# Splitting a matmul burst four and four, and moving ScalarE's exponential ahead of a PSUM bank's emptying, in a graph-attention kernel

## The reference, cut to what matters

```python
def gat_layer(x, graph, W, b):
    h = x @ W
    s = jnp.einsum('bnd,bmd->bnm', h, h) * graph
    s = jnp.where(s == 0.0, NEG_INF, s)
    a = jax.nn.softmax(s, axis=2)
    return jnp.einsum('bnm,bmd->bnd', a, h) + b
heads = jax.vmap(lambda W, b: gat_layer(flow_x, graph, W, b))(Wh, bh)      # 8 heads, 64 -> 128
x = jax.nn.leaky_relu(cat, negative_slope=0.01)                            # cat: the heads side by side
out = gat_layer(x, graph, W_out, b_out)
...
x = _layernorm(x + _L1_gnn_ref(x, adj, L1_gnn_Wh, L1_gnn_bh, L1_gnn_W_out, L1_gnn_b_out), axis=-1)
```

## Time and profile before

| | |
|---|---|
| median of 3 runs | 3353.29 us (3348.22 to 3355.03) |
| profiled execution: its own time, its span | 3351.83 us, 3349.9 us |
| busy: PE, DVE, ACT, POOL | 91%, 87%, 71%, 31% of the span |
| mean granted TensorE clock | 0.976 of full speed |
| the stage of the heads | from the first W product at 386 us to the last at 2101 us |
| DVE idle before L633, in all | 43.2 us, of it 39.8 us until PE's L594 |
| PE idle before L608, in all | 30.8 us, of it 29.6 us until ACT's L672 |
| ACT idle before L831, in all | 163.5 us, all of it until PE's L775 |

### The profile page before, as it was taken

How to read it: one execution, slowest core, us unless ns; L and a number is a source line. 1 busy time by engine, 2 the same in 40 slices (tenths; PEclk the granted TensorE clock), 3 DMA queues, 4 the chain that set the end, 5 groups by cost and what they waited for, 6 DMA issues and landing times. The chain is left out here.

```text
span 3349.9 us, 48846 instructions
## 1 busy us (share of the span) xinstructions
PE 3056.5 (91%) x15035; PEld 1842.5 (55%) x15035; DVE 2925.6 (87%) x3723; ACT 2393.7 (71%) x3653; POOL 1022.2 (31%) x709
## 2 busy tenths in 40 slices
PE   7998899999999999999999999799598888888857
PEld 3676566556665556665656655599454333333323
DVE  3478999999999999999999999688657999999844
ACT  0122688888888888888888888677246999999831
POOL 0123111111111111111111111000125999999821
PEclk9999999999999999999999999899799999999978
DMA  4000000100011111100010111000000000000001
GB/s 98 1 0 1 13 19 19 21 21 19 19 19 19 19 22 19 19 19 19 19 22 19 19 19 19 4 1 0 9 1 0 0 1 1 1 1 0 2 1 25
DMA packets 67230, 46.00 MB, mean 14 GB/s; under 512 B 48464, under 2 KB 49744, under 8 KB 67152
## 3 DMA queue, kind: packets, MB, share of 16 engines
q1 hardware_dynamic: 61920, 43.87, 6.7%
q10 hardware_dynamic: 5232, 1.12, 0.2%
HBM read 42.61 MB, written 2.36 MB: 13 GB/s over the span
## 5 line engine op out<-in xcount | busy, mean ns | idle before, releaser
L661 ACT ACTIVATE hid_work<-hid_work,hid_nmax 128x1024 f32<-128x1024 f32 x512 | 591.1, 1154 | 139.5 <-DVE hid_nmax L645 137.2
L633 DVE TENSOR_TENSOR hid_work<-hid_score_ps,A 128x1024 f32<-128x1024 f32 x512 | 619.5, 1210 | 43.2 <-PE hid_score_ps L594 39.8
L645 DVE CUSTOM_DVE_ANT_0 hid_work<-hid_masks,hid_work 128x1024 f32<-128x1024 f32 x512 | 631.4, 1233 | 0.2 <-DVE hid_masks L653 0.2
L1741 POOL TENSOR_TENSOR el<-el,node_edge 128x1024 f32<-128x1024 f32 x256 | 610.7, 2386 | 18.8 <-DVE el L1723 12.9
L889 POOL TENSOR_TENSOR leaky<-leaky,sloped 128x512 f32<-128x512 f32 x128 | 164.9, 1288 | 1312.5 <-DVE hid_masks L653 1293.5
L608 PE MATMUL hid_turn_ps<-ident,hid_work 128*128 128x128 f32 x4096 | 537.0, 274 | 30.8 <-ACT hid_probsT L672 29.6
L672 ACT COPY hid_probsT<-hid_turn_ps 128x512 f32<-128x512 f32 x1024 | 544.1, 587 | 0.0
L608 PEld LDWEIGHTS hid_turn_ps<-ident,hid_work 128*128 128x128 f32 x4096 | 470.0, 141 | 129.2 <-ACT hid_probsT L672 55.9
L815 PE MATMUL hid_mix_ps<-hid_probsT,x_now 128*64 128x512 f32 x2048 | 495.9, 605 | 1.4 <-ACT hid_probsT L672 1.4
L593 PE MATMUL hid_score_ps<-hid_SX,hid_Y 128*128 (+1 forms) x1024 | 480.5, 469 | 2.6 <-DVE hid_SX L1044 2.6
L594 PE MATMUL hid_score_ps<-hid_SX,hid_Yl 128*128 (+1 forms) x1024 | 406.4, 397 | 0.0
(11 more groups left out here) (280 smaller groups left out, 4100.9 us busy)
## 6 DMA issues: line engine op xcount, KB each, us to landing
hid_r_wide<-hid_r_rows SPq DMA_DIRECT2D x128, 256.0 KB, 4.0
A<-in_adj_dram SPq DMA_DIRECT2D x4, 1024.0 KB, 9.9
X<-in_x_dram SPq DMA_DIRECT2D x8, 256.0 KB, 8.9
hid_r_rows<-hid_rinv SPq DMA_DIRECT2D x128, 2.0 KB, 1.4
out_dram<-X SPq DMA_DIRECT2D x8, 256.0 KB, 3.4
wa<-in_L_gnn_weight_dram ACTq DMA_DIRECT2D x2, 256.0 KB, 14.5
wb<-in_L_gnn_weight_dram ACTq DMA_DIRECT2D x2, 256.0 KB, 14.4
wh<-in_L_gnn_Wh_dram SPq DMA_DIRECT2D x2, 256.0 KB, 5.8
```

The source lines that it names most:

```text
L633: nc.vector.tensor_tensor(work[:, kk % 4, :], score_ps[kk % 2][:], A[:, kk % NT, :], ALU.mult).then_inc(s["weighted"], 1)
L645: nc.vector.tensor_tensor_reduce(work[:, kk % 4, :], masks[:, kk % 2, :], work[:, kk % 4, :], -1.0, 3.0e38, ALU.add, ALU.min, nmax[:, kk % ...
L661: nc.scalar.activation(work[:, kk % 4, :], work[:, kk % 4, :], ACT.Exp, bias=nmax[:, kk % 4:kk % 4 + 1], scale=-1.0, accum_out=rowsum[:, k ...
L1741: nc.gpsimd.tensor_tensor(el[:, q % ELS, :], el[:, q % ELS, :], coefT[:, q // C, :], ALU.mult).then_inc(s_weighted, 1)
```

## The change

Two edits in the stage of the heads. In `pe_burst` the eight matmuls of a group, which stood as six in part 0 and two in part 1, stand as four and four. In `act_step` the exponential is issued ahead of `act_early`, the emptying of the W bank; the order within the other twelve steps of a body is as it was, since `act_early` issues nothing there.

```diff
-                for mt in range(6) if part == 0 else range(6, NT):
+                for mt in range(4 * part, 4 * part + 4):
                     rows = slice(mt % 2 * C, (mt % 2 + 1) * C)
...
             def act_step(act, i, k, first=False, last=False):
                 if k:
                     act_late(act, i, k - 1, first, last)
+                at.act_exp(act, i, k, first, last)
                 act_early(act, i, k, first, last)
-                at.act_exp(act, i, k, first, last)
                 at.act_copy(act, i, k, first, last)
```

## The result

The changed kernel took 3369.58 us (median of 5 runs, 3368.92 to 3370.85), the kernel before 3352.82 us (5 runs, 3348.22 to 3355.03). The ratio is 1.0052, with a 95% interval of 1.0037 to 1.0067: slower by 16.8 us, where 25 us were forecast. The profiled execution took 3370.85 us, its span is 3369.1 us.

The account below looks back on a forecast made before the run. DVE was taken as nearly always at work, waiting only for PE's scores, with PE close to its limit. Four group losses summed to 0.71 to 0.93 us; the middle, 0.82, over 31 bodies gave 25.4 us: 3379 us, range 3346 to 3392.

Parts of the forecast that it names:

- The hold at Y: Steps 0 and 8: PE arrives early at the Y product and waits for L831's later release, about 1 us in step 8.
- ACT's order: Steps 0, 4, 8, 12: exponential at S + 0.12, L831 at S + 1.25, copies at S + 1.84 against 1.79 before.
- S: Start of DVE's mask L653 ahead of steps 0, 4, 8 and 12, the fixed point from which times are counted.
- The start of Y: Step 8's Y product on PE: forecast at S + 1.99, where it stood at S + 1.51 before.
- The end at + 0.22: Step 8's lower end: L633 of step 10 at 7.69 against 7.47, with Y's weights loaded during the wait.
- The signs: What the later profile should show: waits at L762, L874 (0.4 us) and L633, and a body of 55.1 to 55.3 us.
- The move of the burst: Two matmuls, 0.455 us each: 0.91 us moves to ahead of the scores of steps 2, 6, 10 and 14.
- The tails: DVE's work from each group's third L633 to the next S: 6.37, 6.46, 6.32 and 6.51 us.
- the lower end: Sum of the four groups' losses per body without restart cost: 0.11 + 0.12 + 0.22 + 0.26 = 0.71 us.
- The faster rival: W's bank free when PE reaches Y, so L633's waits shrink: 35 us gained, 3318 us; chance 0.13.
- The rival with no change: Loss at Y only replaces PE's present waits: 0.1 or 0.2 us a body, 3353 to 3360 us; chance 0.15.
- the one at 3403 us: ACT also falls behind through late copies in steps 4 and 12: 1.6 us a body, 50 us slower; chance 0.05.

Follow-up runs that it names:

- the split alone: Burst four and four against the kernel before, with ACT's order unchanged: 3315.66 us, ratio 0.9897.
- the nine kernels: The kernel before, the changed kernel and seven follow-up kernels with variants of its two edits; times from 3315.66 to 3462.69 us.
- the kernel with the larger dose: Against the kernel before: burst four and four, and L831 moved behind the exponential and the copies in steps 0 and 8 alone; 3462.69 us, ratio 1.0335.

## Why the prediction was right, and where its sizes were off

**Direction and cause** were right. The hold at Y is there with 0.72 us in step 8 and 0.28 in step 0, it was not there before, and the kernels with and without a Y product behind the moved exponential set it apart: 51 us against 15.

**ACT's order.** Exponential at S + 0.12, L831 at S + 1.26, copies at S + 1.83 (1254.87, 1256.01, 1256.58 against 1254.75); forecast 0.12, 1.25, 1.84. L874 at 3.93 against 3.95, with a wait for L850 as named.

**The start of Y** was put at S + 1.99 with up to 0.11 us for a restart; it was S + 2.08 (1256.83 - 1254.75), and behind it 2.44 us to the burst as without a wait. So the restart's 0.1 us was nearly all there, though ahead of the matmul. The end at + 0.22, which had the weights of Y in place during the wait, would need Y at 1.99. The row of the weight load shows that they were not: it starts with the matmul, not ahead of it.

```profile
1256.82 0.19 PEld L762 LDWEIGHTS hid_misc_ps<-hid_SX,mh_now 128*128 128x128 f32 x1 [0.95 <-issue]
```

**The signs.** PE's wait ahead of L762 in step 8 was to be about 1 us and was 0.72, since PE had waited in step 5; L874 waited 0.26 us for L850, not 0.4. L633 was to wait for PE in steps 2, 6 and 10. Only step 6 has a bracket (0.19 us), but in steps 2 and 10 too L633 starts 0.29 and 0.31 us behind DVE's row ahead of it (L901, at 1290.00 and 1262.17), where 0.09 do without a wait (step 14, 1275.98 to 1276.07): PE came last there, by 0.2 us.

**The move of the burst** was priced too high behind Y: from the burst of step 9 to the turn of step 10 it took 2.91 us (1259.27 to 1262.18), not 2.96, since the price of 0.455 us a matmul was an average over pairs with a fixed part in it: two matmuls took 1.01 us (1246.74 to 1247.75 before), four 1.87, so that a further pair costs 0.86 and not 0.91. In step 8 this and the smaller restart bring 7.80 down to 7.73. In step 4 + 0.12 was forecast and + 0.03 came (6.72): 0.06 of that is this term (1245.20 to 1248.10, 2.90 us). Step 12 came out as forecast, with PE's lost time as the cause.

**The tails** behind the third L633 I had held fixed. They took 6.48, 6.36, 6.36 and 6.48 us instead of 6.37, 6.46, 6.32 and 6.51: + 0.02 in the sum. That they cancel is luck: step 0's was 0.11 longer, step 4's 0.10 shorter. The body therefore grew by 0.71 + 0.02 = 0.73 us, at the lower end of 0.71 to 0.93, not in the middle. That the four groups add up to just the 0.71 of the lower end is chance too: they were 0.16, 0.03, 0.26 and 0.26 where its terms were 0.11, 0.12, 0.22 and 0.26.

**From body to kernel.** 31 times 0.73 is 22.6 us, and the stage grew by just that (1714.7 to 1737.3). The median grew by 16.8. Of the 5.8 us between the two, 3.8 lie behind the stage, where the changed kernel's profiled execution took that much less over the same instructions, and some 2 come from comparing profiled executions with medians (3370.85 against 3369.58 us after, 3351.83 against 3352.82 before). Part of the 3.8 is seen: at the end of the third layer eight matmuls of L1707 took 3.38 us before and 1.94 after, at a granted clock of 0.50 to 0.56 before and 1.00 after. I do not explain the other 2.4 us; the time behind the stage ran from 1243.6 to 1249.1 us over the nine kernels' traces, without relation to the change. A difference of a few microseconds between two kernels is therefore not to be read from one execution of each.

**The faster rival** (the burst's gain comes through) was sized at 35 us, and that is what the split alone gives, in part by luck. Its price was taken from waits of L633 alone, and that of step 0 stayed (0.41 us before and with the split alone); L633's idle time fell by 28.5 us, not 35. Its condition, that the bank of W be free when PE comes, is what the other half of the change takes away. The rival with no change and the one at 3403 us did not come about.

## What to carry to other kernels

Filling an engine's idle time by moving work ahead of a short instruction is not free if that instruction releases something: ask who stands behind the release, not how long the engine idles. ACT's idle time ahead of L831 cost nothing where it was, and removing it cost 54 us of what the other half of the change gained. Two edits in one change are best priced, and tried, apart: here one gave 35 us and the other took more. And a run of instructions that pair up is cut without loss only between pairs.

## What the hardware showed that I had not expected

**Behind a pause of about 2 us PE's clock fell in 19 of 31 bodies.** In the kernel with the larger dose PE stood still for 2.06 us and in 19 of 31 bodies was then granted the lower level for a stretch: 0.50 in the microsecond from 1303, 0.72 in a window of 6 us, score matmuls at a distance of 0.42 us instead of 0.23, some 1.6 us lost each time. In the other 12 the same pause left the clock up, so it does not decide alone; what else does is not shown. The pauses of up to 1.42 us in the same kernel's loop left the time of the group as it was, and in the other kernels, with pauses at Y of up to 1.10 us, the granted clock was 1.00 from 600 to 1900 us. The Trainium skill (TensorE: Matmul & The Clock Gate, section "What's actually happening") says that the throttled clock, 1.2 GHz, is the default and that activity releases it; the two distances, near two to one, and the granted clock of 0.50, agree with its two levels of 1.2 and 2.4 GHz.

**Matmuls into the two halves of a bank's rows run in pairs.** Five cost as much as six (2.72 us), three as much as four (1.86 us). The Trainium skill (TensorEngine Tiling (Array Packing), section "Key Properties") says that different tiles of the array can load and multiply in parallel; that five cost what six cost agrees.
